# A decoder layer on one core: group loads, weight loads and the first input put elsewhere

## The reference

```
x = x + attn(layernorm(x))            # 16 heads of width 16, softmax(q k^T) / sqrt(256) @ v, all 1024 x 1024 scores
x = x + xattn(layernorm(x), ctx)      # 16 heads, 64 context rows per sequence, scores / sqrt(16)
x = x + ffn(layernorm(x))             # weights made ternary by their mean absolute value; 256 -> 1024, exact gelu,
                                      # layernorm over 1024 with weight and bias, 1024 -> 256
```

## Time and profile before

| what | value |
|---|---|
| three runs | 1229.64, 1230.46, 1232.3 us (median 1230.46) |
| profiled execution | 1228.81 us; its span 1226.9 us |
| mean granted clock of TensorE | 0.985 of full speed |
| busy: PE, DVE, ACT, POOL | 94%, 86%, 68%, 24% of the span |
| the chain that ended last, by engine | PE 74%, DVE 15%, issue 3%, ACT 3%, DMA 2%, POOL 1%, SP's queue 1% |
| moved over the span | 74.95 MB, a mean of 61 GB/s |
| first stage, attention stage, last stage | about 0 to 130, 130 to 808, 808 to 1227 us |
| small loads Qs<-mt | 128, in 32 sets of four |

### The profile page before, as it was taken

How to read it: one execution, slowest core, us unless ns; L and a number is a source line. 1 busy time by engine, 2 the same in 40 slices (tenths; PEclk the granted TensorE clock), 3 DMA queues, 4 the chain that set the end, 5 groups by cost and what they waited for, 6 DMA issues and landing times.

```text
span 1226.9 us, 18450 instructions
## 1 busy us (share of the span) xinstructions
PE 1155.1 (94%) x6476; PEld 587.1 (48%) x6476; DVE 1049.5 (86%) x1974; ACT 833.3 (68%) x1386; POOL 294.0 (24%) x404
## 2 busy tenths in 40 slices
PE   5989979999999999999999999998889999999995
PEld 3644333333333333333333333334558677778775
DVE  4688769999999999999999999984699999898875
ACT  4321558877777777777777777774687778778852
POOL 2120301101110110111011000011565465445421
PEclk9999889999999999999999999998999999999998
DMA  4873773303322330430332200023110211100001
GB/s 154 249 229 138 136 168 62 58 15 53 58 39 29 62 54 10 63 57 19 49 58 45 30 11 6 6 69 103 59 35 21 69 61 36 43 18 18 1 18 35
DMA packets 45532, 74.95 MB, mean 61 GB/s; under 512 B 10112, under 2 KB 23296, under 8 KB 45440
## 3 DMA queue, kind: packets, MB, share of 16 engines
q0 software_dynamic: 9792, 27.80, 13.9%
q1 hardware_dynamic: 35648, 45.97, 12.5%
HBM read 47.53 MB, written 25.69 MB: 60 GB/s over the span
## 4 chain that ended last, share of the span: by engine, by line
PE 74%; DVE 15%; issue 3%; ACT 3%; DMA 2%; POOL 1%; SPq 1%; DVEq 0%; ACTq 0%; POOLq 0%
PE ps L1234 21%; PE ps L1353 20%; PE ps L1197 15%; DVE maxes L841 10%; PE ps L1512 4%; PE ps L1432 4%; PE ps L1339 3%; PE ps L1497 2%; PE ps L1441 2%; ACT prob L616 1%; PE ps L1451 1%; DMA Qs<-mt 1%; DVE xhat L1092 1%; DVE maxes L834 1%; PE ps L1401 1%
## 5 line engine op out<-in xcount | busy, mean ns | idle before, releaser
L841 DVE TENSOR_REDUCE maxes<-ps 128x1 f32<-128x512 f32 x968 | 609.2, 684 | 62.9 <-PE ps L1234 62.9
L616 ACT ACTIVATE prob<-ps 128x1024 f32<-128x1024 f32 x512 | 495.8, 1021 | 156.6 <-PE ps L1339 153.8
L1234 PE MATMUL ps<-Ks,Qs 48*128 48x512 f32 x1024 | 364.0, 476 | 17.8 <-DVE maxes L834 2.6
L1234 PEld LDWEIGHTS ps<-Ks,Qs 48*128 48x128 f32 x1024 | 143.6, 184 | 360.0 <-DVE maxes L841 323.6
L1353 PE MATMUL ps<-prob,V_all 128*32 128x512 f32 x2048 | 274.5, 608 | 0.7 <-ACT prob L616 0.6
L1339 PE MATMUL ps<-Qs,Ks 50*128 50x512 f32 x1024 | 239.1, 413 | 9.9 <-DMA Qs<-mt 6.6
L329 POOL DMA_DIRECT2D Qs<-qk_scratch x90 | 44.2, 499 | 494.7 <-PE ps L1353 454.5
L1339 PEld LDWEIGHTS ps<-Qs,Ks 50*128 50x128 f32 x1024 | 134.8, 188 | 26.3 <-ACT prob L616 11.6
L683 ACT ACTIVATE pe_<-ps,nmx 128x64 f32<-128x64 f32 x512 | 109.8, 365 | 8.1 <-DVE nmx L1011 8.0
L540 POOL TENSOR_TENSOR pe_<-pe_,rsum 128x512 f32<-128x512 f32 x64 | 66.6, 1052 | 59.3 <-DVE rsum L1028 59.3
L1512 PE MATMUL ps<-t_p,fT 128*128 128x256 f32 x512 | 76.9, 293 | 0.0
(11 more groups left out here) (116 smaller groups left out, 1238.9 us busy)
## 6 DMA issues: line engine op xcount, KB each, us to landing
qk_scratch<-parts SPq DMA_DIRECT2D x32, 512.0 KB, 3.3
Qs<-qk_scratch POOLq DMA_DIRECT2D x90, 128.0 KB, 5.1
Ks<-qk_scratch POOLq DMA_DIRECT2D x90, 128.0 KB, 7.6
xa<-in_x POOLq DMA_DIRECT2D x8, 512.0 KB, 5.1
o_scratch<-ot SPq DMA_DIRECT2D x128, 32.0 KB
on_raw<-o_scratch SPq DMA_DIRECT2D x8, 512.0 KB
r_raw<-r_scratch SPq DMA_DIRECT2D x16, 256.0 KB
x_in<-in_x SPq DMA_DIRECT2D x8, 512.0 KB, 4.2
```

The costliest lines, as they stand in the source:

```text
L616: act.activation(prob[:, par, h].rearrange("p a q -> p (a q)"), ps[:, 2 * h:2 * h + 2, :].rearrange("p a q -> p (a q)"), ACT.Exp).then_inc ...
L841: dve.tensor_reduce(maxes[:, qc, j * BLK + blk, half:half + 1], ps[:, MAX_BANK["tile", t], :], AX.X, ALU.max).then_inc(max_reduced, 1)
L1234: pe.matmul(ps[:, bank, :], stack(Qs[g], j, STACK, slice(q0, q0 + P)), stack(Ks[g], j, STACK, slice(half * 512, (half + 1) * 512)), start= ...
```

## The change

The first chunk of x is issued on SyncE's queue, ahead of the weights, with a semaphore of its own. GpSimd's loads of groups three and four of the first batch no longer wait for the writes of all chunks. `load_weights` comes in the group G = 2 in place of G = 0, and `abs_part` in steps 72 to 78 in place of 24 to 30. ScalarE sets two of the four `Ks` tiles to one before its wait for the weights and the other two after the copies of the first transposes.

```diff
@@ sync
+            sp.dma_start(xa[:, 0], x_v[0]).then_inc(x_first, 16)
             for n, (t, d) in enumerate(((ident, ident_in), (w_qkv, wqkv.rearrange("(k p) n -> p k n", p=P)),
...
                     m_rows(2 * G + 1, g, 1)
-                    if G == 0:
+                    if G == 2:
                         load_weights()
@@ gpsimd
-            pool.dma_start(xa[:, 0], x_v[0]).then_inc(x_loaded[0], 16)
             pool.dma_start(xa[:, 1], x_v[1]).then_inc(x_loaded[1], 16)
...
-            for m in range(4):
-                pool.wait_ge(parts_written[m], 16 * NCH)
             load_group(pool, 0, 2, group_loaded)
             load_group(pool, 0, 3, group_loaded)
@@ scalar
             act.wait_ge(const_set, 1)
-            for g in range(NG):
+            def key_ones(g):
+
                 act.activation(Ks[g][:].rearrange("p a t -> p (a t)").bitcast(F32R), ones[:, 0:1].broadcast_to([P, 2 * S]),
                                ACT.Copy).then_inc(keys_set, 1)
+
+            key_ones(0)
+            key_ones(1)
             act.wait_ge(a_weights, 16 * 4)
...
             xT_copy(0, 0)
+            key_ones(2)
+            key_ones(3)
             for c in range(NCH):
...
-                if U % 2 == 0 and 24 <= U < 32:
-                    abs_part(U // 2 - 12)
+                if U % 2 == 0 and 72 <= U < 80:
+                    abs_part(U // 2 - 36)
@@ vector
             def a_stats(c):
-                dve.wait_ge(x_loaded[c % 2], 16 * (c // 2 + 1))
+                if c:
+                    dve.wait_ge(x_loaded[c % 2], 16 * ((c + 1) // 2))
+                else:
+                    dve.wait_ge(x_first, 16)
```

More of the change, by code:

```diff
@@ L235, in build @@
         abs_summed = sem("abs_summed")
+        x_first = sem("x_first")
         x_loaded = [sem(f"x_loaded{i}") for i in range(2)]
```

## The result

The changed kernel took 1218.16 us (median of 4 runs, 1215.71 to 1221.43) against 1230.05 (1229.15 to 1232.3): a ratio of 0.9902, 95% interval 0.9875 to 0.993, 11.9 us less. The forecast was 1220.7, in a range of 1217.5 to 1226.0.

A forecast was written before the change was run, and what follows sets the result against it. The matmul engine works nearly everywhere, so only the start and holes in its row can be gained: 8.2 + 2.6 - 1.0 = 9.8 us off 1230.46 gives 1220.7, range 1217.5 to 1226.0.

The forecast's parts named there:

- The hole: Attention stage, second half: 6.64 us matmul wait for maxima rows behind 24 group loads goes, with its slow restart; gain 8.2 us.
- The start: Before the first matmul: first x chunk lands at about 4.9 instead of 7.5 us; gain 2.6 us, bounds 0.5 and 3.3.
- the stretch moves whole: From first transposes to attention stage: nothing waits on a fixed time, so the full 2.6 us gain carries through.
- The collision: First stage, last chunks: parts writes share DMA engines with the earlier 24 loads; loss 1.0 us, bounds 0 and 5.3.
- the reading by which a write would not stand behind the loads at all: DMA engines alternate between queues packet by packet, so parts writes lose nothing to the loads; sum 1.0 us better.
- T: End of the first stage's last rstd, 93.70 us, when GpSimd's queue gets to the 24 group loads.
- The weights: Attention stage, group one to group three: moving the 20 weight issues on SyncE's queue costs 0, bounds 0 and 5 us.
- the clock: Whole kernel: shifts of the clock's dips, left unpriced in the sum; chance 0.04.
- A: First stage: all writes land behind the 24 loads, last chunk's first quarter 5.3 us late; 1225.0 us, chance 0.10.
- D: Second-half boundary: small loads are slow by themselves, the wait stays and only the start is gained; 1228 us, chance 0.03.
- B: Group three: SyncE held by the weights, 5 us lost at the sixth half's maxima rows; 1225.7 us, chance 0.06.
- C: Group three: maxima rows held and landing late behind the weights, 14.6 us lost with slow restart; 1234.3 us, chance 0.04.

The follow-up runs named there:

- the loads alone: Kernel before, with only GpSimd's loads of groups three and four no longer waiting for all writes: 1224.14 us against 1231.21, ratio 0.9944.
- the weights back: Changed kernel with the weights' loads back in group one and the sums of absolute values in steps 24 to 30: 1221.04 us, ratio 0.9934.

## Why the prediction was right

*The hole: 8.2 us, measured 8.2.* Between half one's rows and half five's the changed kernel is 8.23 us shorter, and the loads alone give the same. The cause is shown, not argued: without the weights the hole stays and ends with the loads' last landing, with the small loads on another queue it stays, and with the group loads out of the way it goes.

*The start: 2.6 us, measured 2.76 at the first transposes, but 2.0 where it counts.* The landing was 4.75 (4.9 forecast) and the weights were no wait (b_v landed at 8.9, the transposes began at 9.86). The load took 3.98 us on SyncE's queue; the estimate of 3.2 us rests on a fit that the Trainium skill (DMA: Bandwidth & Descriptors, section Anatomy of one DMA) gives for transfers issued from GpSimd, and it did not hold here. The step that was off is the last sentence of that part, that the stretch moves whole: 0.44 us went in the first chunk, whose first eight `w_qkv` matmuls took 3.78 us in place of 3.38, and 0.3 in the first group's loads, whose last took 8.24 us in place of 7.71.

*The collision: 1.0 us, measured 0.* The mechanism is there: the write of the seventh chunk's first quarter landed 0.4 to 1.3 us after the twentieth load, the last that was issued ahead of it, in all three traces of the changed kernel. So the reading by which a write would not stand behind the loads at all is out. It landed 19.1, 21.2 and 21.7 us after T, where the prediction had 22 to 23, and its need was at T + 23.0: in time, as the prediction's own working said. The 1.0 us on top was a hedge, and nothing paid it. What the prediction missed is that the sixth chunk's fourth quarter is tighter, with 1.1 us to spare in one trace and 0.2 with the weights back. That it cost nothing is in part luck.

*The weights: 0, measured 0* in the trace, SyncE free at 247.8 ("by 250").

*What had no term: the clock.* The prediction gave 0.04 of chance to shifts "that I can't price". The sum of the priced terms was 9.8 and its measured counterpart is 10.2 to 10.4; the rest is the clock's: 3 us in the profiled execution, by the medians 11.9 less 10.2, about 1.7, and over all runs (1231.1 less 1218.3) 2.6. The slow restart behind the hole is in the 8.2. The shift in the last stage is not in any term, and since only kernels without the full hole show it, it seems to come with the change; how is open. The total came out inside the range because this term was small, not because it was foreseen.

*The rivals.* A and D did not happen; B neither, since nothing filled the engines in group three; C's loss does come when the rows are put behind the weights, at 1234.4, but by SyncE's delay alone and not by a slow landing.

## What to carry to other kernels

A burst of loads taken off its wait cost nothing here, but in one trace it left 0.2 us of a margin of nearly 11 us. So ask what small, urgent transfer, and what write whose buffer is needed again, will be issued before the burst has drained, on any queue, and move one of the two. A write issued behind such loads needs a margin of the whole backlog: here it landed 9.5 to 13.4 us after its issue behind 10 to 20 loads of 128 KB, in place of about 3 in the quiet. And where TensorE stands for 2 us at a change of stage, its waits are worth splitting by what each instruction truly reads or overwrites: here the stand was paid twice, once in time and once in clock.

## What the runs showed of the hardware that I had not expected

- Loads of 128 KB into 16 partitions moved at 131 GB/s in the attention stage, with the DMA engines' share at 1.04 (the kernel before, 140 to 145 us). Together with the writes of parts 252 to 346 GB/s were moved (the changed kernel, 94 to 114 us), and the 24 loads were through in 20.5, 23.2 and 24.7 us in its three traces, against 27.1 alone: beside writes they were not slower but faster, by an amount that differs from run to run.
- Four loads of 4 KB each, issued on SyncE's or on ScalarE's queue behind GpSimd's 24, landed only with the end of that backlog (12.41 us): the scores that waited for them started 0.8 us before the last of the 24 had landed in the kernel before, 0.2 after it with the weights alone moved, and 1.5 before it on ScalarE's queue. Behind 20 weight loads of their own queue, the large ones done, they were there within 1.8 us of the last issue.
- The single times of one kernel spread over 12 to 16 us (1216.37 to 1228.01, 1217.63 to 1233.88) and follow the mean granted clock. In the profiled executions the clock falls to its lower level (granted 0.5, 1.2 GHz) at the same few places, but for the program's last few us each time after TensorE had stood for 1.4 us or more. A stand does not always bring it: before, a stand of 2.05 us until 846.34 was followed by the lower clock from 847.5 to 857.8; in the changed kernel's trace the same stand of 2.05 us, until 835.97, was followed by none.
